# A graph layer with LayerNorm: one raw pair per sorting group, 18 held pairs, lane masks on GpSimd, weight splits by slots

## The chip, the cores and the metric

One core of a Trainium2 chip. The time is that of one execution on the device, in microseconds; the kernel before was run three times. VectorE, ScalarE, TensorE, GpSimd and SyncE (which issues most of the DMAs) run their own instruction streams and meet at semaphores.

## What is computed

x has 50000 rows of 256, there are 12500 edges (src, dst, one of 8 relations), dst is sorted:

```python
hx = jnp.einsum('ni,rio->rno', x, weight)
msg = hx[edge_type, src]
agg = jax.ops.segment_sum(msg, dst, num_segments=num_nodes)
node_repr = agg * 0.5 ** 0.5 + h_bias + (x @ loop_weight) * 0.5 ** 0.5
out = layernorm(x + node_repr)
```

## The kernel before

**The work.** x goes through in 98 blocks of 512 rows, two "main pairs" (256 rows) to a block, 196 in all. A pair is turned on TensorE (`turn`), copied from PSUM by ScalarE (`copy_xt`, L1004) and multiplied by the loop weights with identity, mean removal and bias folded in (`multiply`, L1167 and L1176). From pair HOLD on the product is split in three: the copy is rounded (xt_high), VectorE makes the rest (`low`, L788, xt_low), and there are three products of two-part operands. VectorE takes row statistics (L795, L809, L826), ScalarE scales into y_out (L1042), SyncE stores the block.

The edges are sorted by relation into 106 tiles of 128 messages, two to a "message pair", 53 in all. GpSimd gathers their rows of x with indirect DMAs (L562), TensorE turns and multiplies them by the weights of their relation at an offset read from a list, ScalarE moves the result (L1057) through three output buffers, and GpSimd scatters it to a table in the order of the edges (L569). At the end 99 "fix" tiles sum the messages of one node (a matrix of equal keys, L837, times the messages, L1201), gather the raw rows of out (L586), add, normalise and scatter them (L591). Rows with an edge are left unnormalised by the main pairs; a mask of rows without edges (no_edge) sees to that.

**The first stage.** The lists aren't there at the start. 98 columns of edges go through in 14 groups of seven. For each group TensorE does `flag_group` (L1210: lane masks by node lane times columns by node block, which counts the edges of every row) and, two groups later, `sort_group` (L1216, on three masks that VectorE builds in `build_sort`, L750, L752 and L755). ScalarE makes the columns (L1009). The lane masks, seven per group, are made by VectorE for groups 0 to POOL_LANES - 1 (`build_lanes`, L724) and by GpSimd for the rest (L598); `flag_group` on TensorE waits for either. `build_sort(k)` waits until group k - 2 is sorted. Between the groups stand the first HOLD main pairs in raw form: one full product on unrounded data (`first_pair`), moved to y_out by ScalarE (`raw_move`, L1018) and stored unnormalised, since no_edge isn't known yet. `startup`, called by TensorE and ScalarE, writes out this order: two pairs per group step, from step 1 on TensorE and from step 2 on ScalarE.

**The handover.** When the last group is sorted, VectorE reads the list (L765 to L772), which releases GpSimd's gathers. Then it makes the relation offsets (L775 to L778) and, behind ScalarE's copies (L1023), eight low parts of the relation weights (L782), then `low(HOLD)`, `low(HOLD + 1)` and no_edge (L900 to L903). TensorE waits for the offsets before slot HOLD and for all eight splits before the first message pair.

**The slots.** `schedule` lays out the rest in slots that all engines walk: HOLD + LEAD main pairs, then the 53 message pairs with MIXED main pairs among them, PAUSE, and then the remaining main pairs with 92 of the 99 fixes spread over them, and a tail of seven fixes without main pairs. With HOLD 28 and MIXED 74 the message slots begin at slot 32, and the fixes at slot 165, with 84 main pairs beside them. The HOLD // 2 held blocks are read back, normalised and stored again during the message slots, one per three message pairs (`load_late`, `take_held_stats`, `norm_held`, `store_late`). GpSimd's order there is by hand: six message pairs of gathers ahead, then for each pair j the two gathers of j + 6, then the two scatters of j.

Of the kernel before, what the change touches and what calls it, by code (L numbers as in the profile page):

```python
# [7 lines left out]
ALU = mybir.AluOpType  # L8
# [5 lines left out]
AX_X = mybir.AxisListType.X  # L14
# [13 lines left out]
GROUP = 7  # L28
HOLD = 28
LEAD = 4  # L30
MIXED = 74
PAUSE = 6
TAIL = 7
STORE_LATE = 6
POOL_LANES = 8

# [28 lines left out]
def gnn_layernorm_kernel(nc, x, src, dst, rel, weight, bias, loop_weight, out):  # L65
    N, D = x.shape
    E = src.shape[0]
    R = weight.shape[0]
    KT = D // P
# [70 lines left out]
    with ExitStack() as ctx:  # L140
# [266 lines left out]
        def startup(step_f, step_s, step_m, late):  # L407

            for k in range(GROUPS + 4):
                if k < GROUPS:  # L410
                    step_f(k)
                if 2 <= k < GROUPS + 2:
                    step_s(k - 2)
                for m in range(2 * (k - 1 - late), 2 * (k - late)):
                    if 0 <= m < HOLD:
                        step_m(m)

# [233 lines left out]
        def _(dve):  # L651
            steps = [0]

            def link(ins):
                steps[0] += 1
                ins.then_inc(dve_step, 1)
                dve.wait_ge(dve_step, steps[0])
# [100 lines left out]
            for k in range(GROUPS):  # L758
                build_sort(k)
                if k + 2 < POOL_LANES:  # L760
# [12 lines left out]

            ge = rel_ge[0:1, :].rearrange("p (k r) -> p k r", r=R - 1)
            link(nc.vector.tensor_tensor(ge, iota_f[0:1, 0:MTP].unsqueeze(2).broadcast_to([1, MTP, R - 1]),  # L775
                                         start[0:1, 1:R].unsqueeze(1).broadcast_to([1, MTP, R - 1]), ALU.is_ge))
            link(nc.vector.tensor_reduce(rel_n[0:1, :], ge, AX_X, ALU.add))
            nc.vector.tensor_scalar(w_offset[:, :], rel_n[0:1, :], float(KT * D), None, ALU.mult).then_inc(offsets_ready, 1)  # L778
            for part in range(8):
                dve.wait_ge(rel_high, part + 1)  # L780
                at_part = slice(part * PART, (part + 1) * PART)
                nc.vector.tensor_tensor(w_rel_low[:, at_part], w_rel[:, at_part], w_rel_high[:, at_part].bitcast(F32), ALU.subtract).then_inc(rel_split, 1)  # L782

            def low(q):
                if q >= PAIRS or q < HOLD:
                    return
                dve.wait_ge(copied, q + 1)
                nc.vector.tensor_tensor(xt_low[:, q % XT_RING, :], xt_ps[q % 2][:, :], xt_high[:, q % XT_RING, :].bitcast(F32), ALU.subtract).then_inc(low_done, 1)  # L788
# [108 lines left out]
            low(HOLD)  # L897
            low(HOLD + 1)
            dve.wait_ge(flag_grouped, GROUPS)
            nc.vector.tensor_copy(column_f[:, :], flag_ps).then_inc(flags_ready, 1)  # L900
# [6 lines left out]
            for s in range(HOLD, len(slots) + 6):  # L907
# [29 lines left out]
                if s - 1 in late_at:  # L937
                    take_held_stats(late_at[s - 1], 1)
                    aggregate_held(late_at[s - 1])
                prepare_lists(s - LISTS_AT)  # L940

# [51 lines left out]
        def _(act):  # L993
# [89 lines left out]
            startup(flag_group, lambda k: None, raw_move, 1)  # L1083
            for k in range(8):
                split_high(k)

            for s in range(HOLD, len(slots) + 8):
# [5 lines left out]
                if s - 2 in group_end:  # L1093
                    fix_deviation(group_end[s - 2])
                copy_xt(s + 2)
                for f in fs:
                    carry(f)
# [27 lines left out]
        def _(pe):  # L1125
# [105 lines left out]
            startup(flag_group, sort_group, first_pair, 0)  # L1231
            pe.wait_ge(offsets_ready, 1)

            for s in range(HOLD, len(slots)):
# [5 lines left out]
                if kind == "g":  # L1240
                    if n == 0:
                        pe.wait_ge(rel_split, 8)
                    offsets = [pe.value_load(w_offset[0:1, 2 * n + t:2 * n + t + 1], min_val=0, max_val=(R - 1) * KT * D) for t in range(2)]
                if kind != "-":
# [52 lines left out]
```

## Time and profile before

| | us |
|---|---|
| runs | 756.22, 753.68, 757.34 (median 756.22) |
| profiled execution | 756.98 |
| its span | 755.3 |

| engine | busy us | share of the span |
|---|---|---|
| PE | 633.6 | 84% |
| DVE | 553.4 | 73% |
| ACT | 484.2 | 64% |
| POOL | 466.0 | 62% |

PE is TensorE (PEld its weight loads), DVE VectorE, ACT ScalarE, POOL GpSimd. Busy shares are averages over stages with different limits. "<-DVE xt_low" behind an idle time names what ended it; "issue" is a wait for which the profile shows no releaser. A line such as L1144 can stand for many instructions of one helper.

### The profile page before, as it was taken

What the parts mean: (1) busy time and instruction counts of PE and PEld (TensorE: products, weight loads), DVE (VectorE), ACT (ScalarE), POOL (GpSimd) and SP (SyncE); (2) the same over time, 40 slices, a digit from 0 to 9 for tenths busy, and PEclk for the clock granted to TensorE, in tenths of its full rate; (3) what the DMA queues carried; (4) which work ended last, traced back from release to release, by engine and by line L of the source; (5) the groups of instructions that cost most, each with busy time, mean ns of one, the idle gap of its engine ahead of it and who ended that gap; (6) DMA issues with size and microseconds to landing.
All of it is one profiled execution on the core that took longest, in us unless ns stands there. A gap on an engine that the chain in (4) does not pass through costs nothing. (4 is left out here: it accounts for less than half of the span.)

```text
span 755.3 us, 15565 instructions
## 1 busy us (share of the span) xinstructions
PE 633.6 (84%) x4470; PEld 566.6 (75%) x4470; DVE 553.4 (73%) x1843; ACT 484.2 (64%) x1150; POOL 466.0 (62%) x468
## 2 busy tenths in 40 slices
PE   1499999599999998999999999999899888988430
PEld 1378877588888898888989999878787786877310
DVE  4998654776676676767675679989989898889540
ACT  1857875256566666666766567778677777777620
POOL 6980000777777777777775740676776767676273
PEclk9999999799999999999999999999999999999855
DMA  4534455479888888988787589899999999996421
GB/s 146 175 103 131 158 167 169 122 266 335 290 283 300 304 297 307 310 297 289 275 283 223 178 294 291 256 314 319 331 326 297 328 316 331 314 329 211 155 92 41
DMA packets 71393, 187.92 MB, mean 249 GB/s; under 512 B 12890, under 2 KB 28672, under 8 KB 71311
## 3 DMA queue, kind: packets, MB, share of 16 engines
q1 hardware_dynamic: 51727, 139.68, 54.9%
q0 software_dynamic: 19584, 47.23, 19.0%
q8 instruction: 41, 0.67, 0.3%
q14 instruction: 41, 0.34, 0.2%
HBM read 107.60 MB, written 85.59 MB: 256 GB/s over the span
## 5 line engine op out<-in xcount | busy, mean ns | idle before, releaser
L788 DVE TENSOR_TENSOR xt_low<-xt_ps,xt_high 128x512 fp32r<-128x512 f32 x221 | 151.4, 685 | 91.3 <-ACT xt_high L1004 88.6
L1176 PE MATMUL y_ps<-w_high,xt_high 128*128 128x256 f32 x672 | 190.8, 284 | 0.0
L1176 PE MATMUL y_ps<-w_high,xt_low 128*128 128x256 f32 x672 | 190.5, 284 | 0.0
L1176 PE MATMUL y_ps<-w_low,xt_high 128*128 128x256 f32 x672 | 190.4, 283 | 0.0
L562 POOL DMA_INDIRECT gathered<-in_x,src_at x105 | 112.9, 1075 | 110.6 <-DVE edge_at L772 78.9
L1004 ACT ACTIVATE xt_high<-xt_ps 128x512 fp32r<-128x512 f32 x221 | 130.2, 589 | 40.0 <-PE xt_ps L1144 39.3
L591 POOL DMA_INDIRECT out_rows<-y_fix,fix_at x99 | 99.0, 1000 | 73.9 <-ACT y_fix L1076 51.0
L1042 ACT ACTIVATE y_out<-y_ps,rstd 128x256 f32<-128x256 f32 x336 | 138.9, 467 | 3.4 <-DVE rstd L826 3.2
L1144 PE MATMUL xt_ps<-ident,x_in 128*128 128x128 f32 (+1 forms) x784 | 118.8, 275 | 25.5 <-DMA x_in<-in_x 15.8
L1176 PEld LDWEIGHTS y_ps<-w_high,xt_low 128*128 128x128 f32 x672 | 128.6, 191 | 7.5
L569 POOL DMA_INDIRECT message_rows<-message_out,edge_at x105 | 106.2, 1012 | 43.3 <-issue 28.1
L1176 PEld LDWEIGHTS y_ps<-w_low,xt_high 128*128 128x128 f32 x672 | 129.2, 192 | 1.0
L1176 PEld LDWEIGHTS y_ps<-w_high,xt_high 128*128 128x128 f32 x672 | 129.0, 192 | 0.0
L586 POOL DMA_INDIRECT y_fix<-out_rows,fix_at x99 | 100.6, 1016 | 43.2 <-issue 42.5
L795 DVE BATCH_NORM_STATS2 stats<-y_ps 128x6 f32<-128x256 f32 x336 | 126.4, 418 | 0.0
L1144 PEld LDWEIGHTS xt_ps<-ident,x_in 128*128 128x128 f32 (+1 forms) x784 | 92.9, 142 | 28.5 <-issue 25.8
L1201 PE MATMUL y_ps<-message_in,same 128*128 128x256 f32 x198 | 66.7, 420 | 40.7 <-DVE y_fix L844 21.3
L1167 PE MATMUL y_ps<-bias_rows,ones_r 128*128 128x512 f32 x196 | 99.3, 506 | 0.9 <-ACT y_out L1042 0.7
L1028 ACT ACTIVATE std<-masked,eps 128x4 f32<-128x4 f32 x84 | 24.8, 295 | 93.8 <-DVE masked L812 92.0
L1176 PE MATMUL y_ps<-w_rel_low,xt_high 128*128 x212 | 65.1, 307 | 20.4 <-issue 14.2
L1201 PEld LDWEIGHTS y_ps<-message_in,same 128*128 128x128 f32 x198 | 30.9, 196 | 55.2 <-issue 54.6
L1076 ACT ACTIVATE y_fix<-y_fix,fix_shift,fix_rstd 128x256 f32<-128x256 f32 x99 | 53.5, 591 | 18.9 <-DVE fix_shift L866 18.9
(166 smaller groups left out, 1069.7 us busy)
## 6 DMA issues: line engine op xcount, KB each, us to landing
x_in<-in_x SPq DMA_DIRECT2D x97, 512.0 KB, 5.1
out_rows<-y_out SPq DMA_DIRECT2D x97, 512.0 KB
message_in<-message_rows SPq DMA_DIRECT2D x99, 128.0 KB
column_of<-out_rows SPq DMA_DIRECT2D x14, 512.0 KB
out_rows<-column_of SPq DMA_DIRECT2D x14, 512.0 KB, 3.9
keys<-key_table SPq DMA_DIRECT2D x12, 512.0 KB, 6.4
w_rel<-in_L_gnn_weight SPq DMA_DIRECT2D x1, 2048.0 KB, 13.5
gathered<-in_x,src_at POOLq DMA_INDIRECT x105, 4.5
```

Source lines behind the costliest of these rows:

```text
L562: nc.gpsimd.indirect_dma_start(gathered[:, c % (2 * ROWS_RING), :], None, x, bass.IndirectOffsetOnAxis(ap=src_at[:, c:c + 1], axis=0), bou ...
L569: nc.gpsimd.indirect_dma_start(message_rows, bass.IndirectOffsetOnAxis(ap=edge_at[:, c:c + 1], axis=0), message_out[:, c % (2 * OUT_RING), ...
L586: nc.gpsimd.indirect_dma_start(y_fix[:, i % FIX_RING, :], None, out[0:rows, :], bass.IndirectOffsetOnAxis(ap=fix_at[:, i:i + 1], axis=0), ...
L591: nc.gpsimd.indirect_dma_start(out, bass.IndirectOffsetOnAxis(ap=fix_at[:, i:i + 1], axis=0), y_fix[:, i % FIX_RING, :], None, bounds_chec ...
L788: nc.vector.tensor_tensor(xt_low[:, q % XT_RING, :], xt_ps[q % 2][:, :], xt_high[:, q % XT_RING, :].bitcast(F32), ALU.subtract).then_inc(l ...
L795: last = nc.vector.bn_stats(stats[:, ln_slot(b), 2 * (m % 2) + t, :], product_tile(m_at[m], t))
L1004: nc.scalar.activation(to, xt_ps[q % 2][:, :], ACT.Copy).then_inc(copied, 1)
L1042: last = nc.scalar.activation(y_tile(m, t), product_tile(m_at[m], t), ACT.Copy, scale=rstd[:, ln_slot(b), i:i + 1])
L1144: last = nc.tensor.transpose(xt_ps[q % 2][:, at_column:at_column + parts], rows[t][:, k * P:(k + 1) * P], ident[0:parts, 0:parts])
L1167: nc.tensor.matmul(y_ps[bank[q]][:, :], ones_r[:, :], bias_rows[:, :], start=True, stop=False)
L1176: return nc.tensor.matmul(to, xt[:, at_row:at_row + P], w, start=start, stop=stop)
L1201: nc.tensor.matmul(f_tile(i), same[:, i % WINDOW_RING, :], message_in[:, i % WINDOW_RING, :], start=True, stop=True).then_inc(f_product, 1)
```

## The change

HOLD falls from 28 to 18 and MIXED rises from 74 to 78, so message slots begin at slot 22 and fix slots at 159, with 90 main pairs beside the same 92 fixes; nine held blocks are left of 14. In the first stage pairs 0 and 1 come ahead of group 0 on TensorE, pairs 2 and 3 behind it, then one pair per group (ScalarE one step later). VectorE makes the lane masks of four groups, GpSimd those of ten. The relation offsets stand behind `low(HOLD)` and `low(HOLD + 1)`, the splits of the relation weights two by two in slots 18 to 21 on ScalarE and VectorE, and TensorE waits for the offsets only at the first message pair.

```diff
--- before.py
+++ after.py
@@ -26,13 +26,13 @@
 FIX_RING = 16
 WINDOW_RING = 8
 GROUP = 7
-HOLD = 28
+HOLD = 18
 LEAD = 4
-MIXED = 74
+MIXED = 78
 PAUSE = 6
 TAIL = 7
 STORE_LATE = 6
-POOL_LANES = 8
+POOL_LANES = 4
 
 
 def schedule(mains, messages, fixes):
@@ -406,14 +406,18 @@
 
         def startup(step_f, step_s, step_m, late):
 
-            for k in range(GROUPS + 4):
-                if k < GROUPS:
+            for k in range(-1, GROUPS + 4):
+                if 0 <= k < GROUPS:
                     step_f(k)
                 if 2 <= k < GROUPS + 2:
                     step_s(k - 2)
-                for m in range(2 * (k - 1 - late), 2 * (k - late)):
-                    if 0 <= m < HOLD:
-                        step_m(m)
+                for m in raw_pairs(k - late):
+                    step_m(m)
+
+        def raw_pairs(k):
+            if k < 1:
+                return [2 * k + 2, 2 * k + 3] if k >= -1 else []
+            return [k + 3] if k + 3 < HOLD else []
 
         def needs_repair(eng):
             eng.wait_ge(flag_ready, 1)
@@ -771,12 +775,7 @@
             link(nc.vector.tensor_scalar(empty[:, :], found_edge[:, :], 0.0, float(SKIP), ALU.is_equal, ALU.mult))
             nc.vector.tensor_tensor(edge_at[:, :], found_edge[:, :], empty[:, :], ALU.add).then_inc(list_ready, 1)
 
-            ge = rel_ge[0:1, :].rearrange("p (k r) -> p k r", r=R - 1)
-            link(nc.vector.tensor_tensor(ge, iota_f[0:1, 0:MTP].unsqueeze(2).broadcast_to([1, MTP, R - 1]),
-                                         start[0:1, 1:R].unsqueeze(1).broadcast_to([1, MTP, R - 1]), ALU.is_ge))
-            link(nc.vector.tensor_reduce(rel_n[0:1, :], ge, AX_X, ALU.add))
-            nc.vector.tensor_scalar(w_offset[:, :], rel_n[0:1, :], float(KT * D), None, ALU.mult).then_inc(offsets_ready, 1)
-            for part in range(8):
+            def split_low(part):
                 dve.wait_ge(rel_high, part + 1)
                 at_part = slice(part * PART, (part + 1) * PART)
                 nc.vector.tensor_tensor(w_rel_low[:, at_part], w_rel[:, at_part], w_rel_high[:, at_part].bitcast(F32), ALU.subtract).then_inc(rel_split, 1)
@@ -896,6 +895,11 @@
 
             low(HOLD)
             low(HOLD + 1)
+            ge = rel_ge[0:1, :].rearrange("p (k r) -> p k r", r=R - 1)
+            link(nc.vector.tensor_tensor(ge, iota_f[0:1, 0:MTP].unsqueeze(2).broadcast_to([1, MTP, R - 1]),
+                                         start[0:1, 1:R].unsqueeze(1).broadcast_to([1, MTP, R - 1]), ALU.is_ge))
+            link(nc.vector.tensor_reduce(rel_n[0:1, :], ge, AX_X, ALU.add))
+            nc.vector.tensor_scalar(w_offset[:, :], rel_n[0:1, :], float(KT * D), None, ALU.mult).then_inc(offsets_ready, 1)
             dve.wait_ge(flag_grouped, GROUPS)
             nc.vector.tensor_copy(column_f[:, :], flag_ps).then_inc(flags_ready, 1)
             dve.wait_ge(flags_ready, 1)
@@ -937,6 +941,9 @@
                 if s - 1 in late_at:
                     take_held_stats(late_at[s - 1], 1)
                     aggregate_held(late_at[s - 1])
+                if s < HOLD + 4:
+                    for part in range(2 * (s - HOLD), 2 * (s - HOLD) + 2):
+                        split_low(part)
                 prepare_lists(s - LISTS_AT)
 
             with dve.If(needs_repair(dve)):
@@ -1081,8 +1088,6 @@
             copy_xt(1)
             act.wait_ge(nodes_ready, 2)
             startup(flag_group, lambda k: None, raw_move, 1)
-            for k in range(8):
-                split_high(k)
 
             for s in range(HOLD, len(slots) + 8):
                 kind, n, fs = at_slot(s)
@@ -1093,6 +1098,9 @@
                 if s - 2 in group_end:
                     fix_deviation(group_end[s - 2])
                 copy_xt(s + 2)
+                if s < HOLD + 4:
+                    for part in range(2 * (s - HOLD), 2 * (s - HOLD) + 2):
+                        split_high(part)
                 for f in fs:
                     carry(f)
                 if s - 2 in block_end and s - 2 >= HOLD:
@@ -1229,7 +1237,6 @@
             nc.tensor.matmul(misc_ps[:, 0:R], upper[:, :], count[:, :], start=True, stop=True)
             nc.tensor.matmul(misc_ps[:, R:2 * R], ones[:, :], count[:, :], start=True, stop=True).then_inc(counts_summed, 1)
             startup(flag_group, sort_group, first_pair, 0)
-            pe.wait_ge(offsets_ready, 1)
 
             for s in range(HOLD, len(slots)):
                 kind, n, fs = slots[s]
@@ -1240,6 +1247,7 @@
                 if kind == "g":
                     if n == 0:
                         pe.wait_ge(rel_split, 8)
+                        pe.wait_ge(offsets_ready, 1)
                     offsets = [pe.value_load(w_offset[0:1, 2 * n + t:2 * n + t + 1], min_val=0, max_val=(R - 1) * KT * D) for t in range(2)]
                 if kind != "-":
                     multiply(s, offsets)
```

## Rows read from the trace of the kernel before

**Rows 1.** Busy time by stage; PE, PEld, DVE, ACT, POOL (count), PEclk, DMA share, GB/s

```profile
62.00:117.00 55.00, 55.00 (x320) 44.26 (x318) 35.77 (x32) 44.70 (x88) 0.00 (x0) 1.00 0.49 153
162.00:400.00 238.00, 220.17 (x1748) 211.16 (x1747) 162.78 (x555) 157.62 (x375) 180.88 (x177) 0.99 0.86 296
450.00:705.00 255.00, 233.17 (x1602) 203.96 (x1601) 229.72 (x904) 187.57 (x489) 165.33 (x164) 1.00 0.91 304
```

**Rows 2.** Timeline of TensorE: one group of the first stage, then the handover

```profile
61.17 1.34 PE L1210 MATMUL y_ps<-column_of,y_fix 128*128 128x394 f16 x7
...
65.69 0.60 PE L1144 MATMUL xt_ps<-ident,x_in 128*128 128x128 f32 x4
...
68.09 1.17 PE L1210 MATMUL y_ps<-column_of,y_fix 128*128 128x394 f16 x6
...
139.97 1.09 PE L1144 MATMUL xt_ps<-ident,x_in 128*128 128x128 f32 x4 [9.65 <-DVE xt_low L788]
```

**Rows 3.** Timeline of ScalarE in the same group (start us, us, engine, line)

```profile
61.87 3.69 ACT L1009 ACTIVATE column_of<-work 128x394 f16<-128x394 f32 x7
65.47 0.58 ACT L1004 ACTIVATE message_out<-xt_ps 128x512 f32<-128x512 f32 x1
65.94 0.58 ACT L1018 ACTIVATE y_out<-y_ps 128x512 f32<-128x512 f32 x1
```

**Rows 4.** Timeline of VectorE: sorting work and lane masks of the first stage

```profile
44.13 0.92 DVE L750 TENSOR_TENSOR gathered<-work 128x742 f16<-128x742 f16 x1
44.97 1.17 DVE L752 TENSOR_TENSOR keys<-work 128x896 f16<-128x896 f16 x1
46.07 2.46 DVE L755 TENSOR_TENSOR gathered<-gathered,work 128x2226 f16<-128x2226 f16 x1
48.45 1.29 DVE L724 TENSOR_SCALAR y_fix<-work 128x128 f16<-128x128 f16 x7
...
57.43 1.08 DVE L752 TENSOR_TENSOR keys<-work 128x896 f16<-128x896 f16 x1
```

**Rows 5.** GpSimd's lane masks: ns min/median/max; up to 44.1 us, then 43.45 to 54.45

```profile
L598 POOL TENSOR_SCALAR message_in<-work x30: 595/708/3501, 15.1 to 44.1; 128x128 f16<-128x128 f16 x30
L598 POOL TENSOR_SCALAR y_fix<-work x8: 593/594/819, 10.3 to 14.3; 128x128 f16<-128x128 f16 x8
...
L598 POOL TENSOR_SCALAR message_in<-work x4: 707/1044/3499, 43.4 to 48.9; 128x128 f16<-128x128 f16 x4
L598 POOL TENSOR_SCALAR same<-work x2: 1392/2446/3501, 49.6 to 51.0; 128x128 f16<-128x128 f16 x2
```

**Rows 6.** Timeline of VectorE, then of GpSimd, at the handover to the message stage

```profile
130.36 0.49 DVE L765 CAST work<-y_ps 128x318 int32<-128x318 f32 x1 [7.03 <-PE y_ps L1216]
...
132.31 0.92 DVE L775 TENSOR_TENSOR work<-work 1x742 f32<-1x742 f32 x1
...
134.34 4.89 DVE L782 TENSOR_TENSOR w_rel_low<-w_rel,w_rel_high 128x512 fp32r<-128x512 f32 x8
...
134.91 5.21 POOL L562 DMA_INDIRECT gathered<-in_x,src_at  x1 [0.30 <-issue]
...
157.43 1.02 POOL L569 DMA_INDIRECT message_rows<-message_out,edge_at  x1 [1.63 <-ACT message_out L1057]
```

**Rows 7.** GpSimd's groups by line, 162 to 400 us: busy, mean ns, idle before

```profile
L562 POOL DMA_INDIRECT gathered<-in_x,src_at x89 | 92.3, 1037 | 27.1 <-issue 23.8 <-PE xt_ps L1144 1.8 <-ACT message_out L1057 1.5
L569 POOL DMA_INDIRECT message_rows<-message_out,edge_at x88 | 89.2, 1013 | 30.2 <-issue 24.7 <-ACT message_out L1057 4.3 <-PE xt_ps L1144 1.2
```

**Rows 8.** VectorE's groups by line in the fix stage, 450 to 705 us

```profile
L795 DVE BATCH_NORM_STATS2 stats<-y_ps 128x6 f32<-128x256 f32 x169 | 63.6, 418 | 0.0
L788 DVE TENSOR_TENSOR xt_low<-xt_ps,xt_high 128x512 fp32r<-128x512 f32 x83 | 56.3, 678 | 13.5 <-ACT xt_high L1004 13.1
...
L809 DVE BATCH_NORM_AGGREGATE mean_var<-stats 128x2 f32<-128x6 f32 x168 | 16.0, 157 | 1.1
...
L826 DVE RECIPROCAL rstd<-std 128x4 f32<-128x4 f32 x42 | 7.6, 181 | 0.0
```

## The prediction

> **What bounds the kernel now.** I read three stretches of the stage table first [rows 1], then the order of work of each engine inside them. In the first stage TensorE is busy for all of 55 us, GpSimd does nothing, and the DMA engines are half used. One group takes TensorE 68.09 - 61.17 = 6.92 us, of which the second of its two raw pairs is 68.09 - 65.69 = 2.40 us [rows 2]. So this stage is a pure TensorE queue, 14 groups long, and ends when VectorE reads the sorted list at 130.36 [rows 6]. The second stage (messages) looks like TensorE too (220 of 238 us), but it is not: GpSimd issues indirect DMAs back to back, each followed by 0.3 us of "issue". 89 + 88 of them with their gaps fill 92.3 + 27.1 + 89.2 + 30.2 = 238.8 us, all of the window [rows 7]. That is 1.35 us each, four per message pair, 5.4 us per pair for 53 pairs, however many main pairs stand between. TensorE has 238 - 220 = 18 us of room there [rows 1]. The third stage (fixes) has VectorE busy 229.7 of 255 us, with TensorE, the DMA share (0.91) and GpSimd all close behind [rows 1]. So a microsecond off the first stage moves the whole GpSimd queue forward; a main pair added to the second stage is nearly free; one added to the third is paid.
>
> **First stage.** By the new order pairs 0 and 1 go ahead of group 0, pairs 2 and 3 behind it, then one per group, up to 18. Per group TensorE needs 6.92 - 2.40 = 4.52 us [rows 2]. ScalarE needs seven column tiles, 65.47 - 61.87 = 3.60, one copy of a turned tile, 65.94 - 65.47 = 0.47, and one raw move that costs as much, so 4.55 us [rows 3]. VectorE needs the three sorting operations, 48.45 - 44.13 = 4.32 us; its seven lane masks per group stop after group 3 instead of group 7 [rows 4]. All three come out at 4.3 to 4.6, so I take 4.5 us per group. The chain of groups starts in earnest at 44.1: VectorE's orders for groups 0 to 3 are unchanged, and it finishes the lanes of group 3 when it starts its next sorting work at 44.13 [rows 4]. Before that point the three more raw pairs (7.2 us) fall into time in which TensorE waited for VectorE. Group 13 is then flagged at 44.2 + 10 x 4.5 = 89.2; behind it come its own step (4.5), one sort with the last pair and a last sort (about 4.5). GpSimd left out, the stage would end at 98.2.
>
> GpSimd isn't out of it. It now builds 70 lane masks, not 42. The first eight took 0.594 us each, which is a mask alone [rows 5]. Up to 44.1 it has finished 37 (8 + 30, the last just starting [rows 5]). While VectorE works without a pause, masks take 0.71, 1.39 and 3.50 us in turn, six of them in about 11 us. Two of VectorE's 5.5 us cycles hold these six, and the long ones lie across its large multiply of 46.07 to 48.45 [rows 4, 5]. The cheap mask of each three falls in the time of the seven small lane operations, which are gone in the new cycle of 4.3 us. So I take two masks per group time, 2.25 us each, as the likeliest price beside sorting work, and 0.6 where VectorE waits. TensorE wants groups 11, 12 and 13 at 80.2, 84.7 and 89.2, and for them 56, 63 and 70 masks. At 80.2 there are 37 + 2 x 36.1 / 4.5 = 53. The missing three come about 3.9 us late. From there on VectorE must wait for TensorE too, so of seven masks two are made beside 4.3 us of sorting and five alone in 3.0. A group then takes 7.4 us instead of 4.5, 2.9 late twice. Sum 3.9 + 2.9 + 2.9 = 9.7, and the stage ends at 107.9 instead of 130.36: **22.5 us saved**. Bounds: masks at 0.6 throughout, 98.2, 32.2 saved; no mask at all finished beside sorting work, so that seven times 0.6 is added to each 4.3 from group 9 on, about 120.6, 9.8 saved.
>
> The Trainium skill ("SBUF — State Buffer", section "SBUF: two separate sides") says that the port pair which VectorE and GpSimd share is locked for a whole instruction and that the loser fully blocks. Read as one mask passed at each end of a VectorE operation, that would give three masks in 4.5 us; the stage would end near 100.8 and the saving would be 29.6. The masks of 3.50 us agree with blocking, but one of them spans two operation ends, so this trace doesn't agree with that reading of it.
>
> **The handover.** Today the lists are followed by the relation offsets (2.0 us from 132.31 to 134.34) and the eight splits of the relation weights (4.89 us) before the first low part, and TensorE stands still for 9.65 us [rows 2, 6]. The change puts the offsets behind two low parts and two splits into each of the next four slots, on VectorE and on ScalarE. VectorE then has before the first message product: two low parts 1.4, offsets 2.0, flag columns about 1.6, four slots at 1.7 plus 1.2 of splits, together about 16 to 17 us after the lists. TensorE's added waits (offsets, all eight splits) hold only its own queue there. GpSimd, which sets the end of this stage, needs 14 gathers before its first scatter, 14 x 1.35 = 19 us, so the splits are covered; without that cover they would cost up to 7 us. What GpSimd gains is only its own: the second gather took 5.21 us beside the splits, 4.2 more than the usual 1.04 [rows 6, 7], and 1.63 was waited for the first message [rows 6]. The split pairs, 1.2 us each, can still hold up four gathers by as much. Between 0 and 5.8 I take **3 us saved**. That TensorE idles less and may keep its granted clock counts nothing, since GpSimd is behind.
>
> **Message stage.** 78 main pairs instead of 74: 4 x 2.40 = 9.6 us of TensorE into 18 us of room [rows 1, 2]. Nine held blocks instead of 14 are read back, normalised and written, ten transfers of 512 KB fewer; also covered. Since ScalarE, TensorE and GpSimd wait for one another through three output buffers, I charge **1 us** (0 to 9.6).
>
> **Fix stage.** Of the ten pairs that left the first stage six land here: 90 slots instead of 84 for the same 92 fixes. A main pair costs VectorE 56.3 / 83 + 63.6 / 84.5 + (16.0 + 7.6) / 84 = 0.68 + 0.75 + 0.28 = 1.71 us [rows 8]. At a busy share of 229.7 / 255 = 0.90 that is 1.9 us, six are **11 us more**. Bounds: 10 by the bare work, 6 x 255 / 84 = 18 if a slot costs the same with fewer fixes in it. Bytes say the same: 6 x 0.52 MB at 304 GB/s is 10 us. The tail behind the last main pair doesn't change.
>
> **Sum.** -22.5 - 3 + 1 + 11 = -13.5 us. The profiled execution took 756.98 us (span 755.3 and 1.7 around it), so 743.5; it lies 0.8 above the median 756.22, so the median should be **742.7**.
>
> **Rivals.**
> A, GpSimd is hardly late. With masks at 0.6 us the stage ends at 98.2 and the time is 742.7 - 9.7 = 733.0; with three masks in 4.5 us there are 67 of 70 at 89.2, only group 13 waits, about 2.6, and it is 735.6. The second is what the rule of the page above would give. For it: median 0.71 us over 30 masks; against: the pattern of 3.50. Chance 0.2.
> B, the gain is eaten later: fix slots cost 18, the message stage its 9.6, or masks finish at only one per sorting cycle (114, 6 more). Any one gives 749 to 751. Chance 0.2.
> C, the port is paid by VectorE: each mask blocks it for 0.6 us. From 44.1 VectorE has 12 x 4.32 + 33 x 0.6 = 72 us, the last sort is near 118, 12.4 saved, time 752.8. The same section of the Trainium skill says the lock works both ways. Against it: with a mask passing, VectorE's operation takes 1.17 us, alone 1.08 [rows 4]. Chance 0.08.
> D, the other side: GpSimd's masks never speed up when VectorE waits. 33 masks at 2.25 end at 118.4 and with 8.8 us behind it the stage at 127.2; 3.1 saved, -3.1 - 3 + 1 + 11 = +5.9, time 762. It decides from about 2.1 us per mask. Against it: 0.594 wherever VectorE is quiet [rows 5]. Chance 0.04.
> The forecast itself (738 to 747) has 0.48.
>
> **The numbers.** About 0.5% (3.8 us, 752.4) is what a measurement of this kernel can tell. A, B and the forecast lie below it, C on it, D above. Faster 0.86, same 0.09, slower 0.05. The range takes in most of A and B: 733 to 752.
>
> **What would show it.** One group of the first stage at 4.5 us of TensorE, then three groups at 7 to 8 with TensorE waiting for GpSimd's lane masks; if these waits are missing, A. The sorted list read near 108. Masks between 44 and 80 at 2.2 us on average; VectorE's sorting operations not longer than now. Splits in pairs between low parts, no gather of 5 us, the first scatter some 22 us after the list. 5.4 us per message pair as before. 90 fix slots at about 2.95 us, some 266 us in place of 255. A fix stage over 270, or message pairs over 5.5, would make the sum wrong; so would a list later than 115.

## The result, and the profile after

The changed kernel takes 744.94 us (median of 4 runs, 743.72 to 746.04), the kernel before 755.75 beside it; the ratio is 0.9858, with a 95% interval of 0.9828 to 0.9888. So it is faster by 1.4%; forecast were 742.7 us and 1.8%. The profiled execution has a span of 743.8 us.

For the comparison I cut each execution at the same six events. In this and the table further down "list" is the moment VectorE starts to read the sorted list, and the other columns are the times from one event to the next: to GpSimd's first scatter, to its last scatter, to the first matmul of a fix, to the last bias matmul of a main pair, and to the end of the span. The event times are rounded to 0.1 us before they are subtracted.

| kernel | list | to first scatter | to last scatter | to first fix | to last main pair | tail | span |
|---|---|---|---|---|---|---|---|
| before | 130.4 | 27.0 | 280.3 | 12.5 | 253.1 | 52.0 | 755.3 |
| after | 110.5 | 25.8 | 285.1 | 12.3 | 258.3 | 51.8 | 743.8 |
| difference | -19.9 | -1.2 | +4.8 | -0.2 | +5.2 | -0.2 | -11.5 |
| forecast | -22.5 | -3 | +1 | 0 | +11 | 0 | -13.5 |

First the stages after, as in [rows 1]: busy us (and instructions) of PE, PEld, DVE, ACT, POOL, then the granted clock of TensorE, the DMA share and GB/s.

```profile
62.00:101.00 39.00, 30.50 (x159) 21.54 (x157) 27.26 (x20) 27.64 (x54) 36.43 (x28) 0.87 0.26 76
142.00:380.00 238.00, 222.46 (x1786) 214.24 (x1784) 156.99 (x522) 150.38 (x355) 178.05 (x174) 1.00 0.83 278
433.70:692.00 258.30, 247.06 (x1690) 213.76 (x1688) 237.68 (x931) 194.00 (x507) 165.16 (x164) 1.00 0.94 313
```

The end of the first stage now has TensorE at 30.5 of 39 us with a granted clock of 0.87, where it was full before, and GpSimd at work. The message stage and the fix stage look as before, with TensorE at 247 of 258 us in the latter (233 of 255 before).

TensorE's timeline of the changed kernel shows where the first stage lost its pace (L1218 is `flag_group`; start us, us; in brackets the idle time and what ended it).

```profile
66.08 1.35 PE L1218 MATMUL y_ps<-column_of,y_fix 128*128 128x394 f16 x7
...
70.64 0.34 PE L1218 MATMUL y_ps<-column_of,y_fix 128*128 128x394 f16 x1
70.82 1.17 PE L1218 MATMUL y_ps<-column_of,message_in 128*128 128x394 f16 x6
...
79.44 2.46 PE L1218 MATMUL y_ps<-column_of,message_in 128*128 128x394 f16 x7 [4.10 <-POOL message_in L602]
...
85.45 1.34 PE L1218 MATMUL y_ps<-column_of,message_in 128*128 128x394 f16 x7
...
94.54 2.46 PE L1218 MATMUL y_ps<-column_of,message_in 128*128 128x394 f16 x7 [4.40 <-ACT column_of L1016]
...
101.51 1.00 PE L1218 MATMUL y_ps<-column_of,message_in 128*128 128x394 f16 x5
...
109.39 1.12 PE L1224 MATMUL y_ps<-gathered,keys 128*128 128x318 f16 x7
113.32 1.09 PE L1152 MATMUL xt_ps<-ident,x_in 128*128 128x128 f32 x4 [2.81 <-DVE xt_low L787]
```

Groups 8 and 9 start 4.56 us apart, as forecast (4.5). Group 10 waits 4.10 us for GpSimd's masks, and then its seven matmuls take 2.46 us instead of 1.34: after the wait TensorE has its lower clock, 1.2 instead of 2.4 GHz (granted clock 0.50 from 79.44 to 81.7 us, 1.00 from 66 to 75). Group 11 follows at once, group 12 waits 4.40 us and is slow again, group 13 doesn't wait. (The second wait is put down to ScalarE's columns, but the columns that ended at 94.40 are those of group 13; group 12's were done at 89.84, and GpSimd's 63rd mask, the last that group 12 needs, ended at 94.39.)

GpSimd's masks (L602, ns min/median/max) in four of VectorE's sorting cycles, 56.75 to 74.1 us, and VectorE's timeline beside the last of them:

```profile
L602 POOL TENSOR_SCALAR message_in<-work x6: 1952/3341/3502, 56.7 to 70.7; 128x128 f16<-128x128 f16 x6
```

```profile
69.43 0.92 DVE L754 TENSOR_TENSOR gathered<-work 128x742 f16<-128x742 f16 x1
70.27 1.17 DVE L756 TENSOR_TENSOR keys<-work 128x896 f16<-128x896 f16 x1
71.36 2.46 DVE L759 TENSOR_TENSOR gathered<-gathered,work 128x2226 f16<-128x2226 f16 x1
...
83.26 0.93 DVE L754 TENSOR_TENSOR gathered<-work 128x742 f16<-128x742 f16 x1 [5.01 <-PE y_ps L1224]
...
98.89 0.93 DVE L754 TENSOR_TENSOR gathered<-work 128x742 f16<-128x742 f16 x1 [6.69 <-PE y_ps L1224]
```

Six masks in 17.4 us, 1.95, 3.34 and 3.50 us in turn, three in 8.8 us: 1.5 masks per cycle of sorting work (4.4 us), not the two that I took. The second block shows the cycle without a gap (0.84, 1.09 and 2.4 us from start to start), and that VectorE later waits 5.01 and 6.69 us for TensorE, which is when GpSimd catches up.

The handover on VectorE and on GpSimd, as in [rows 6], and two rows of TensorE's timeline there:

```profile
110.54 0.49 DVE L769 CAST work<-y_ps 128x318 int32<-128x318 f32 x1 [2.24 <-PE y_ps L1224]
...
113.69 0.91 DVE L899 TENSOR_TENSOR work<-work 1x742 f32<-1x742 f32 x1
...
117.91 1.28 DVE L781 TENSOR_TENSOR w_rel_low<-w_rel,w_rel_high 128x512 fp32r<-128x512 f32 x2
...
116.40 1.33 POOL L566 DMA_INDIRECT gathered<-in_x,src_at  x1 [0.30 <-issue]
118.04 1.42 POOL L566 DMA_INDIRECT gathered<-in_x,src_at  x1 [0.31 <-issue]
...
136.35 1.06 POOL L573 DMA_INDIRECT message_rows<-message_out,edge_at  x1 [2.73 <-ACT message_out L1064]
...
123.81 1.11 PE L1152 MATMUL xt_ps<-ident,gathered 128*128 128x128 f32 x4 [2.48 <-DMA gathered<-in_x,src_at]
...
130.06 0.38 PE L1184 MATMUL y_ps<-w_rel_low,xt_high 128*128 x1 [2.11 <-DVE xt_low L787]
```

The splits (L781) come two by two, and the gathers beside them take 1.20 to 1.48 instead of 1.00 us; none takes 5. (The gather of 1.33 us at 116.40 stands ahead of the splits, beside the operations that make no_edge.) But GpSimd then waits 2.73 us for the first message, where it waited 1.63 before: TensorE waits 2.48 us for gathered rows, turns them at its lower clock (1.11 us for four), waits 2.11 for VectorE, and begins the first message product at 130.06. TensorE's wait after the last sort fell from 9.65 us [rows 2] to 2.81.

GpSimd in a window of the message stage as long as that of [rows 7], then VectorE in the fix stage as in [rows 8]:

```profile
L566 POOL DMA_INDIRECT gathered<-in_x,src_at x86 | 89.2, 1037 | 26.2 <-issue 24.4 <-PE xt_ps L1152 1.5 <-ACT message_out L1064 0.3
L573 POOL DMA_INDIRECT message_rows<-message_out,edge_at x88 | 89.1, 1013 | 33.7 <-issue 25.3 <-ACT message_out L1064 7.3 <-PE xt_ps L1152 1.2
```

```profile
L794 DVE BATCH_NORM_STATS2 stats<-y_ps 128x6 f32<-128x256 f32 x180 | 67.6, 417 | 0.0
L787 DVE TENSOR_TENSOR xt_low<-xt_ps,xt_high 128x512 fp32r<-128x512 f32 x89 | 60.4, 679 | 16.1 <-ACT xt_high L1011 15.7
L843 DVE SCALAR_TENSOR_TENSOR y_fix<-y_fix,raw_scale,y_ps 128x256 f32<-128x256 f32 x89 | 40.8, 460 | 1.3 <-DMA y_fix<-out_rows,fix_at 1.3
```

174 DMAs in 238 us instead of 177, because GpSimd waits 7.3 + 0.3 us for messages (ScalarE's moves, L1064) instead of 4.3 + 1.5, and some more behind "issue". In the fix stage VectorE's work per main pair is what [rows 8] have, but its wait for gathered rows is 1.3 us. Before the change the same row, from first fix to last main pair, was:

```profile
L844 DVE SCALAR_TENSOR_TENSOR y_fix<-y_fix,raw_scale,y_ps 128x256 f32<-128x256 f32 x89 | 41.0, 465 | 8.8 <-DMA y_fix<-out_rows,fix_at 8.7
```

### The profile page after: what moved, and what is told of

It is laid out like the page before. It is cut to its first block and busy times, and to the rows that moved or that the text cites. A ratio compares the mean times of both kernels' runs of the same rounds, so it can differ in the third digit from the quotient of the medians.

```text
span 743.8 us, 15650 instructions
## 1 busy us (share of the span) xinstructions
PE 637.3 (86%) x4510; PEld 567.8 (76%) x4510; DVE 555.1 (75%) x1825; ACT 476.6 (64%) x1140; POOL 507.3 (68%) x496
## 3 DMA queue, kind: packets, MB, share of 16 engines
q0 software_dynamic: 19584, 47.23, 20.1%
## 5 line engine op out<-in xcount | busy, mean ns | idle before, releaser
L787 DVE TENSOR_TENSOR xt_low<-xt_ps,xt_high 128x512 fp32r<-128x512 f32 x231 | 158.2, 685 | 101.6 <-ACT xt_high L1011 100.1
L1184 PE MATMUL y_ps<-w_high,xt_high 128*128 128x256 f32 x712 | 202.2, 284 | 0.0
L1184 PE MATMUL y_ps<-w_low,xt_high 128*128 128x256 f32 x712 | 201.9, 284 | 0.0
L1184 PE MATMUL y_ps<-w_high,xt_low 128*128 128x256 f32 x712 | 201.8, 283 | 0.0
L1011 ACT ACTIVATE xt_high<-xt_ps 128x512 fp32r<-128x512 f32 x231 | 135.9, 588 | 45.8 <-PE xt_ps L1152 45.6
L1049 ACT ACTIVATE y_out<-y_ps,rstd 128x256 f32<-128x256 f32 x356 | 146.9, 466 | 0.1
L566 POOL DMA_INDIRECT gathered<-in_x,src_at x105 | 110.5, 1053 | 46.8 <-issue 29.6
L1184 PEld LDWEIGHTS y_ps<-w_high,xt_low 128*128 128x128 f32 x712 | 136.3, 191 | 7.9
L573 POOL DMA_INDIRECT message_rows<-message_out,edge_at x105 | 106.3, 1012 | 49.1 <-issue 29.6
L1184 PEld LDWEIGHTS y_ps<-w_low,xt_high 128*128 128x128 f32 x712 | 136.9, 192 | 0.7
L1184 PEld LDWEIGHTS y_ps<-w_high,xt_high 128*128 128x128 f32 x712 | 136.4, 192 | 0.0
L794 DVE BATCH_NORM_STATS2 stats<-y_ps 128x6 f32<-128x256 f32 x356 | 133.6, 417 | 0.0
L1209 PE MATMUL y_ps<-message_in,same 128*128 128x256 f32 x198 | 67.2, 422 | 31.7 <-ACT message_in L1072 17.4
L1035 ACT ACTIVATE std<-masked,eps 128x4 f32<-128x4 f32 x89 | 26.3, 295 | 105.2 <-DVE masked L811 102.2
L1184 PE MATMUL y_ps<-w_rel_low,xt_high 128*128 x212 | 65.5, 309 | 20.1 <-issue 14.9
```

The costliest lines, as they stand in the source:

```text
L566: nc.gpsimd.indirect_dma_start(gathered[:, c % (2 * ROWS_RING), :], None, x, bass.IndirectOffsetOnAxis(ap=src_at[:, c:c + 1], axis=0), bou ...
L573: nc.gpsimd.indirect_dma_start(message_rows, bass.IndirectOffsetOnAxis(ap=edge_at[:, c:c + 1], axis=0), message_out[:, c % (2 * OUT_RING), ...
L794: last = nc.vector.bn_stats(stats[:, ln_slot(b), 2 * (m % 2) + t, :], product_tile(m_at[m], t))
L1011: nc.scalar.activation(to, xt_ps[q % 2][:, :], ACT.Copy).then_inc(copied, 1)
L1049: last = nc.scalar.activation(y_tile(m, t), product_tile(m_at[m], t), ACT.Copy, scale=rstd[:, ln_slot(b), i:i + 1])
L1184: return nc.tensor.matmul(to, xt[:, at_row:at_row + P], w, start=start, stop=stop)
```

## The experiments

Each ran beside the kernel before on the same chip, whose median there was 756.83 to 759.68 us; ratios are to that, so kernels are best compared by them. Cuts as in the table above. They come from one profiled execution of each kernel, and executions of equal work differ: from first to last scatter the six kernels with MIXED 78 and HOLD 18 take 282.9 to 285.3 us, and the 84 fix slots 253.1 in the kernel before but 256.9 in e4, whose slots are the same.

| kernel | time | ratio (95%) | list | to first scatter | to last scatter | to last main pair, from first fix | span |
|---|---|---|---|---|---|---|---|
| after | 744.94 | 0.9858 (0.9828 to 0.9888) | 110.5 | 25.8 | 285.1 | 258.3 | 743.8 |
| e1 POOL_LANES 8 | 736.21 | 0.9717 (0.9675 to 0.9759) | 102.3 | 25.6 | 285.3 | 258.7 | 736.5 |
| e2 POOL_LANES 6 | 739.90 | 0.9767 (0.9725 to 0.9810) | 105.2 | 26.3 | 283.8 | 258.7 | 738.5 |
| e9 POOL_LANES 7 | 735.64 | 0.9701 (0.9666 to 0.9736) | 101.5 | 26.2 | 285.3 | 258.2 | 735.5 |
| e3 splits put back | 744.90 | 0.9833 (0.9788 to 0.9878) | 110.4 | 26.6 | 282.9 | 259.0 | 743.1 |
| e4 before, POOL_LANES 4 | 758.19 | 1.0008 (0.9983 to 1.0032) | 129.3 | 27.0 | 281.0 | 256.9 | 758.7 |
| e5 before, MIXED 68 | 752.43 | 0.9939 (0.9918 to 0.9959) | 129.3 | 27.6 | 271.0 | 257.8 | 750.0 |
| e6 MIXED 74 | 746.44 | 0.9855 (0.9824 to 0.9887) | 109.3 | 26.0 | 278.8 | 264.8 | 744.2 |
| e7 MIXED 84 | 752.74 | 0.9938 (0.9915 to 0.9962) | 109.5 | 25.8 | 292.5 | 254.2 | 747.3 |
| e10 fixes bunched | 756.17 | 0.9997 (0.9971 to 1.0023) | 109.7 | 25.0 | 284.8 | 272.7 | 753.7 |
| e8 HOLD 16 | 739.86 | 0.9754 (0.9716 to 0.9791) | 101.0 | 26.8 | 287.6 | 260.5 | 741.2 |
| e11 lanes 7, MIXED 76 | 731.88 | 0.9650 (0.9614 to 0.9686) | 100.8 | 24.8 | 280.4 | 259.0 | 728.1 |

### Who sets the first stage: the lane masks (e1, e2, e9, e4)

```diff
-POOL_LANES = 4
+POOL_LANES = 8
```

> The changed kernel with POOL_LANES 8, so that VectorE makes the lane masks of eight groups and GpSimd those of six (42 masks, as before). Theory, GpSimd's late masks set the first stage: TensorE waits for no lane mask any more, keeps its clock, and the list is read at about 102 to 103 us instead of 110.5 (VectorE's own sorting work is then the longest row); the time falls by 8 us to about 737. Rival, the loop between ScalarE and TensorE or VectorE's three sorting operations set it: the waits move to another releaser and the list stays at 108 to 111, time 743 to 746.

The list is read at 102.3, and the ratio goes from 0.9858 to 0.9717. From group 8 on TensorE waits for nothing and keeps its clock (timeline of this kernel, start us, us):

```profile
66.08 1.34 PE L1218 MATMUL y_ps<-column_of,y_fix 128*128 128x394 f16 x7 [0.68 <-DVE y_fix L728]
...
70.60 1.34 PE L1218 MATMUL y_ps<-column_of,y_fix 128*128 128x394 f16 x7
...
79.66 1.34 PE L1218 MATMUL y_ps<-column_of,message_in 128*128 128x394 f16 x7
...
84.18 1.34 PE L1218 MATMUL y_ps<-column_of,message_in 128*128 128x394 f16 x7
...
88.73 1.35 PE L1218 MATMUL y_ps<-column_of,message_in 128*128 128x394 f16 x7
...
93.29 1.01 PE L1218 MATMUL y_ps<-column_of,message_in 128*128 128x394 f16 x5
```

What is left is VectorE, 0.7 to 0.8 us late in each of the groups for which it makes masks, as the 0.68 in the first row. The rival falls: ScalarE's loop with TensorE allows 4.5 us per group. The time is 736.2, where 737 was expected.

```diff
-POOL_LANES = 4
+POOL_LANES = 6
```

> The changed kernel with POOL_LANES 6 (56 masks on GpSimd, 14 more lane operations on VectorE, 2.4 us in all). Theory: at 1.5 masks per 4.5 us beside sorting work GpSimd is late only for group 13, by some 3 us, and VectorE's additional 2.4 us fit into its slack; list read at 101 to 103, time 736. Rival (GpSimd isn't the cause): list at 108 to 111, time 743 to 746.

Only group 13 is late (its wait was named 3 us, it is 3.77), and TensorE is slow behind it. The list came at 105.2, 2 us later than I had it, and the time is 739.9, not 736:

```profile
94.47 1.46 PE L1218 MATMUL y_ps<-column_of,message_in 128*128 128x394 f16 x5 [3.77 <-POOL same L602]
```

```diff
-POOL_LANES = 4
+POOL_LANES = 7
```

> The changed kernel with POOL_LANES 7 (49 masks on GpSimd). With 56 masks on GpSimd the last group was 3.8 us late, with 42 VectorE was late by 0.7 to 0.8 us in each of groups 3 to 7. Theory: with 49 the last masks come before group 13 is due at about 91 us, VectorE is late in one group fewer; list at 101 to 102, time 735 to 737. Rival: GpSimd is late again for group 13, list 104 to 106, time 739 to 740.

The list is read at 101.5 and no group waits for GpSimd: the theory holds. 7 and 8 can't be told apart (intervals 0.9666 to 0.9736 and 0.9675 to 0.9759); both are better than the change's 4, by 9 us in the medians and 11 to 12 by the ratios.

> The kernel before with POOL_LANES 4 alone (still two raw pairs per group, 28 held). VectorE waits 2.6 us in each group of 6.92 us there, in which GpSimd's masks take 0.6 us. Theory: GpSimd makes some six masks per group beyond group 8 and has its 70 ready long before group 13 is due at 116 us; TensorE never waits for them; time as before, 755 to 757. Rival, ten groups of masks on GpSimd are slow by themselves: TensorE waits for lane masks and the time rises by over 4 us.

The other side of it, the kernel before with the ten groups of masks alone (edit `POOL_LANES = 8` to 4): no difference, ratio 1.0008. The same masks on the same engine, but beside a VectorE that waits 2.6 us in every 6.92 (L598, window 56 to 83 us, ns min/median/max):

```profile
L598 POOL TENSOR_SCALAR message_in<-work x23: 596/601/2585, 55.8 to 82.3; 128x128 f16<-128x128 f16 x23
```

The median is 601 ns where it is 3341 in the changed kernel. So ten groups of masks aren't slow by themselves. Packing VectorE's sorting work makes them slow, and that came with the second raw pair's removal. The two parts of the change that are each harmless alone cost some 9 to 12 us together. How much of that is the waits for masks and how much the lower clock behind them isn't told apart.

### The handover (e3)

```diff
+            for part in range(8):
+                split_low(part)
             low(HOLD)
             low(HOLD + 1)
-            ge = rel_ge[0:1, :].rearrange("p (k r) -> p k r", r=R - 1)
...
-                if s < HOLD + 4:
-                    for part in range(2 * (s - HOLD), 2 * (s - HOLD) + 2):
-                        split_low(part)
```

(The offsets go back ahead of the splits, ScalarE's half likewise, and TensorE waits for the offsets ahead of slot HOLD.)

> The changed kernel with the relation offsets and all eight splits ahead of the first low part again, as before the change. Theory, GpSimd's own queue sets this place: TensorE stands still some 10 us after the last sort instead of 3.9, one gather takes over 4 us, and the first scatter comes 27 us after the list is read instead of 25.8; time 1 to 2 us more, 746 to 747. Rival, TensorE's standstill counts: 6 to 7 us more, 751 to 752.

```profile
119.99 1.09 PE L1150 MATMUL xt_ps<-ident,x_in 128*128 128x128 f32 x4 [9.65 <-DVE xt_low L792]
...
114.92 5.21 POOL L566 DMA_INDIRECT gathered<-in_x,src_at  x1 [0.31 <-issue]
...
137.03 1.02 POOL L573 DMA_INDIRECT message_rows<-message_out,edge_at  x1 [1.21 <-ACT message_out L1063]
```

TensorE again stands still for 9.65 us and one gather takes 5.21, and the time is the same: 744.90, intervals overlapping. I had expected 1 to 2 us more; the first scatter comes 0.8 us later after the list, and the message stage is 2.2 us shorter (282.9 against 285.1), no more than executions of equal work differ. GpSimd waits 1.21 us for the first message here and 2.73 in the changed kernel. The first matmul of xt_low with relation weights starts at 130.5 here and 130.3 there: TensorE begins its four slots 6.7 us earlier in the changed kernel and loses them again, to VectorE's splits between the low parts and to the wait for gathered rows. The move of the splits and offsets is worth nothing that can be measured: the intervals leave room for the 1 to 2 us that I expected, not for the rival's 6 to 7.

### Where main pairs are cheap (e5, e6, e7)

```diff
-MIXED = 74
+MIXED = 68
```

> The kernel before with MIXED 68 alone: six main pairs move from the message stage to the fix stage (90 slots, 2 of them with two fixes, instead of 84 with 8). Theory, slots with two fixes cost some 2 us more than others with what follows them: the fix stage takes 258 us instead of 253, as in the changed kernel, and the message stage some 1 to 3 us less; time 757 to 760. Rival, my price of 11 us for six pairs by VectorE's busy time over its share: fix stage 264, time 764 to 766.

A miss in my favour: 0.9939. The fix stage took 257.8 us as expected, not 264, so my price falls. But the message stage fell by 9.3 us, from 280.3 to 271.0, for six pairs, where I had written 1 to 3.

> The changed kernel with MIXED 74: four main pairs fewer beside the messages, 94 fix slots, none with two fixes. Theory: message stage from first to last scatter back from 285 to about 281 us, since GpSimd is late for want of messages less often; fix stage 94 slots at 2.9, 14 instead of 17 above 258, so 268 to 271; time 749 to 753. Rival, the message stage doesn't depend on its main pairs: it stays at 285 and the time is 754 to 757.

> The changed kernel with MIXED 84: six main pairs more beside the messages, 84 fix slots of which 8 hold two fixes, as before the change. Theory: the fix stage goes back to 253 us (5 less); the message stage has too little room on TensorE for six more pairs at 2.1 us and grows by 6 to 10 us; time 746 to 750. Rival, GpSimd still sets the message stage: it stays at 285 us and the time is 740.

With the changed kernel at 74, 78 and 84 pairs the message stage takes 278.8, 285.1 and 292.5 us: 1.4 us for each pair over the whole range, and 1.55 in e5 (one execution each). In e6 the stage is 6.3 us shorter (expected 4) and the fix stage 6.5 longer, so the time is 746.4, below what I expected, and level with the change. In e7 it is 752.7, above what I expected, though its fix stage (254.2) and its message stage (7.4 us more) are as expected; the profiled execution, 749.5, is one of its shortest. In e7's stretch from first scatter to last gather TensorE is nearly full, and GpSimd waits 19.5 us for messages:

```profile
135.30:391.60 256.30, 243.50 (x1955) 234.84 (x1954) 172.66 (x573) 162.63 (x385) 186.78 (x182) 1.00 0.82 279
...
POOL message_rows L573 <- ACT message_out L1064: 19.5, 14, 2.7
```

So the message stage has no flat part to hide pairs in. Where the pairs are paid shows when the stage is cut at GpSimd's last gather, which lies some 35 us before its last scatter (TensorE, VectorE and the rest as in [rows 1]; the kernel before, then the changed one):

```profile
157.40:402.90 245.50, 226.53 (x1797) 217.24 (x1797) 168.52 (x573) 160.55 (x382) 186.60 (x183) 0.99 0.86 295
402.90:437.70 34.80, 33.25 (x269) 32.46 (x270) 20.06 (x59) 20.84 (x49) 21.25 (x22) 1.00 0.62 210
```

```profile
136.30:385.70 249.40, 232.54 (x1867) 223.96 (x1866) 163.13 (x539) 157.15 (x370) 186.58 (x182) 1.00 0.83 280
385.70:421.40 35.70, 34.54 (x281) 33.55 (x280) 22.45 (x69) 20.62 (x48) 21.31 (x22) 1.00 0.62 199
```

| kernel, MIXED | to last gather | of it GpSimd waits for ScalarE's messages | last gather to last scatter |
|---|---|---|---|
| e5, 68 | 242.3 | 5.8 | 28.7 |
| before, 74 | 245.5 | 7.5 | 34.8 |
| e6, 74 | 244.2 | 6.7 | 34.6 |
| after, 78 | 249.4 | 10.3 | 35.7 |
| e7, 84 | 256.3 | 20.1 | 36.2 |

In the last part TensorE is busy for all but 1 to 2 us and GpSimd isn't, so there TensorE sets the pace; of the 9.3 us that e5 saves, 6.1 lie there. But between before and after, and from e6 to e7, that part hardly changes (0.9 and 1.6 us). Nearly all the rest, 3.9 us for the four pairs of the change and 12.1 for the ten from e6 to e7, comes earlier, while GpSimd still has gathers to issue: it waits longer for messages, although TensorE still has 13 to 19 us of room. I take it that each unevenness of the order makes one of the two wait for the other; no run shows that by itself.

### The fix stage (e10)

```diff
-        until = (m + 1 - first) * (fixes - TAIL) // rest
+        until = min((m + 1 - first) * (fixes - TAIL) // (rest - 6), fixes - TAIL)
```

> The changed kernel with its 92 fixes spread over the first 84 of the 90 main pairs of the fix stage (8 slots with two fixes, the last 6 with none) instead of over all 90 (2 slots with two). Main pairs and fixes in the stage are the same in number. Theory, a slot with two fixes costs about 2 us above one with one, with what follows it: the first 84 slots take what they took before the change, 253 to 257 us, six main pairs alone 2.1 us each, together 266 to 270 instead of 258; time 752 to 757. Rival, only the sum of VectorE's work counts: 258 to 260, time 744 to 747.

Nothing but the spacing differs, and it costs 14.4 us of the stage (2.7 come back in the tail, 49.1 instead of 51.8) and 11 of the time. The time, 756.2, is in the range expected; the stage, 272.7, is 3 us above its range. The miss is in the last six main pairs, which have no fixes: by the bias products on TensorE the first 84 take 255.4 us, as expected, and these six 17.3 us, no less than the last six of the changed kernel with their fixes (17.1). So a main pair took 2.9 us there with or without a fix beside it. VectorE's wait for gathered rows is back at the level of the kernel before:

```profile
L843 DVE SCALAR_TENSOR_TENSOR y_fix<-y_fix,raw_scale,y_ps 128x256 f32<-128x256 f32 x92 | 42.2, 464 | 9.6 <-DMA y_fix<-out_rows,fix_at 9.6
```

The starts of xt_low on VectorE tell the same. In the changed kernel they repeat 3.57, 2.27, 3.22, 2.43 us (2.87 on average) up to its first slot with two fixes, the 45th; behind it a second pattern of 2.95 us. A slot with two fixes takes 2.8 to 5.3 us in the kernel before, and the pattern jumps at each and at some slots between (4.25, 4.58). So the stage's 5.2 us for six more main pairs are not 0.9 us per pair. They are six more slots at 2.9 us, less what six doubled slots and their late gathers had cost: 17.4 - 12.2. The 5.2 is a figure of two single executions: against e4, which ran the slots of the kernel before in 256.9 us with 11.4 us of waits for gathered rows, it would be 1.4. The stages of 90 evenly spaced slots agree better (257.8 to 259.0, but 260.5 in e8).

### Fewer held pairs, and the best of them (e8, e11)

> POOL_LANES 8, HOLD 16 and MIXED 80 on the changed kernel: two raw pairs fewer in the first stage, two main pairs more beside the messages, the fix slots unchanged. By the runs so far a pair costs 2.4 us of TensorE in the first stage and about 1.5 us beside the messages: list read at 97.5 to 99.5 us (102.3 with HOLD 18), message stage from first to last scatter 288 us (285.3), time 1 to 3 us below the same kernel with HOLD 18, 733 to 735. Rival, the pairs at the end of the first stage stood beside sorting work and the message stage charges more, as from 78 to 84 pairs: time 737 to 740.

The edit is HOLD 16 and MIXED 80 on e1. It missed: 739.9, not better than e1 (by median 3.7 us worse, but the intervals overlap). The list comes only 1.3 us earlier, because VectorE's last sorting masks are now what TensorE waits for:

```profile
98.96 2.04 PE L1224 MATMUL y_ps<-gathered,keys 128*128 128x318 f16 x7 [3.27 <-DVE gathered L759]
```

and the seven matmuls behind that wait take 2.04 instead of 1.12 us. The message stage is 2.3 us longer for its two pairs. The fix stage is 1.8 us longer although its slots are the same; the profiled execution is the slowest of the four (743.3 us), so that part may be scatter.

```diff
-MIXED = 78
+MIXED = 76
...
-POOL_LANES = 4
+POOL_LANES = 7
```

> The changed kernel with POOL_LANES 7 and MIXED 76: 92 main pairs beside 92 fixes, one to one, and two main pairs fewer beside the messages. By the runs so far a main pair costs about 1.5 us beside the messages, so the message stage falls by 3 us (285 to 282); the fix stage of 90 slots takes 258 us and that of 94 265, so 92 slots 260 to 262 and no slot with two fixes is left; sum 0 to -2 us against POOL_LANES 7 alone, 733 to 736. Rival, the fix stage charges the full 2.9 us for each slot: 264, time 738.

731.88 us, ratio 0.9650, better than both kernels and 1 us below the range that I expected; the interval just overlaps that of e9, 0.9666 to 0.9736. 92 main pairs beside 92 fixes take 259.0 us; VectorE no longer waits for gathered rows at all, and the four-slot pattern of 2.87 us holds to the end:

```profile
L787 DVE TENSOR_TENSOR xt_low<-xt_ps,xt_high 128x512 fp32r<-128x512 f32 x91 | 62.3, 684 | 12.1 <-ACT xt_high L1011 10.8
L843 DVE SCALAR_TENSOR_TENSOR y_fix<-y_fix,raw_scale,y_ps 128x256 f32<-128x256 f32 x90 | 41.5, 461 | 0.1
```

## Why the prediction was right, and where it wasn't

**The first stage** was the right place and the right mechanism: 4.5 us per group in step with the 4.56 measured, groups held up at the end by GpSimd's masks, 19.9 us saved instead of 22.5. The step that was mis-sized is "I take two masks per group time". It was 1.5, 2.93 us each. I had three masks in a cycle of 5.5 us and took away only the cheap one. But without the small lane operations a cycle has three ends of VectorE operations, and every mask from 44.5 to 76.2 us lasted past two of them. With 1.5 the same working gives a first wait at group 10, where it was; there were two waits of over 4 us, at groups 10 and 12, and not three. I had also left out that TensorE comes back from such a wait at half its clock: 2.46 instead of 1.34 us for seven matmuls, twice. The reading of the lock as one mask per operation end (100.8) is refuted by these masks and by the list at 110.5, and e1, e2 and e9 show that the masks are what set it. Rival C, VectorE paying for each mask, falls too: its operation beside a mask took 1.17, as in [rows 4], and e1, with 28 fewer masks on GpSimd, runs its groups no faster than 4.5 us. Rival D falls by e4 and by the masks of 0.6 us while VectorE waited.

**The handover** was sized 3 us and is 1.2 in the cut, and nothing by e3. The failed step is "GpSimd needs 14 gathers before its first scatter, so the splits are covered": by count it holds (14 gathers ended at 133.6), but the first message came later, and the first scatter at 136.35. I had TensorE at the first message product 16 to 17 us after the lists (112.6); it was 17.5, and I had left out the product itself, at the lower clock, and ScalarE's move behind it, over 5 us more.

**The message stage** is where the reasoning, not only a size, was wrong. "However many main pairs stand between" is refuted by e5, e6 and e7: 1.4 to 1.55 us per pair. I charged 1 us, it was 4.8 for four pairs. The step that failed is taking GpSimd's queue as full because its DMAs and gaps fill the window of [rows 7]. Of those gaps 4.3 + 1.5 us were waits for ScalarE's messages and 1.8 + 1.2 for TensorE, so GpSimd wasn't alone in setting the pace, and the waits for messages grow with the pairs, up to the last gather from 5.8 us with 68 pairs to 20.1 with 84. That the window ends at 400 us and leaves out the last 38 us, where TensorE sets the pace, matters for e5 but gives only 0.9 of the 4.8.

**The fix stage** was charged 11 us and took 5.2 (1.4 against e4's execution of the old slots). VectorE's busy time did grow by 9.8 us (227.9 to 237.7), near the 10 of the bare work. The step that failed is dividing it by the busy share, as if waits grew along. They shrank, since eight slots with two fixes became two. e10 shows that by undoing the spacing alone.

The sum came out 2 us off because these errors cancel: +2.6 (masks), +1.8 (handover), +3.8 (messages), -5.8 (fixes), and -0.4 in the rest. That the sum came so near is luck: two of the four terms were off by 4 to 6 us, in opposite directions, and the reasoning behind one of them was wrong.

What stays open: why GpSimd's lane masks need two ends of VectorE operations and not one. The durations fit that, no run measured it by itself. Nor is it shown why a main pair beside messages costs 1.4 us before TensorE is full, why a main pair of the fix stage took 2.9 us even without a fix, or how the 12.2 us divide between late gathers and the doubled slots themselves.

## What to carry to other kernels

When two parts of a change each use the slack of the same engine, cost them together: the masks were free while VectorE waited, and the other part took that waiting away. A queue that fills a window isn't the only limit if some of its gaps are waits for other engines: here these waits grew from 7.5 to 10.3 and 20.1 us as main pairs were added. And a stage can be bound by another engine at its end, so read it up to its last instruction before calling extra work free. Even spacing can matter as much as the amount of work: the same main pairs and fixes, bunched into fewer slots, took 11 us more.

## What the runs showed of the hardware

A GpSimd tensor_scalar of 128x128 fp16 takes 0.6 us while VectorE waits, and 1.95 to 3.50 us beside back-to-back VectorE tensor_tensor operations with two SBUF inputs; from 44.5 to 76.2 us each of them ended 0.38 to 0.39 us after the second end of a VectorE operation behind its own start. Of the VectorE operations the one of 1.08 us takes 1.17 meanwhile (1.26 once). The Trainium skill ("SBUF — State Buffer", section "SBUF: two separate sides") says that whoever holds the shared pair makes the other wait for the whole instruction. The trace agrees for GpSimd in that its masks wait for VectorE operations to end, but they lasted past two of them, not one. For VectorE it doesn't agree: no operation of it was held for the 0.6 us of a mask.

Indirect gathers issued by GpSimd grow too, to 5.21 us beside eight VectorE subtractions in a row and to between 1.20 and 1.48 beside two, from 1.00.

After waits of 4.10 and 4.40 us TensorE ran at 1.2 GHz (granted clock 0.50, seven matmuls in 2.46 us), and after 2.81 us at the handover as well (0.50 from 113.32 to 116.5 us, the four turns in 1.09 instead of 0.60 us).
